# Window attention at one core: exponential out of PSUM, K spread by GpSimd, 32-column tiles, both pairs of windows weighed at once

## What is computed

```python
xn = layernorm(x)                         # over the 96 channels of a pixel
xw = windows(roll(xn, -4, -4))            # 4 windows of 8 x 8 = 64 tokens per image
q, k, v = split(xw @ qkv_w + qkv_b)       # 12 heads of 8 channels
attn = q * SCALE @ k.T + rel_bias + shift_mask     # 64 x 64 per window and head
out = softmax(attn) @ v                   # 12 heads side by side: 96 channels
x = x + unroll(out @ proj_w + proj_b)
```

## Time and profile before

| | before |
|---|---|
| time, median of 3 runs | 535.92 us |
| lowest and highest | 535.07, 537.8 us |
| profiled execution: span from first to last instruction | 540.4 us |
| TensorE busy | 518.1 us, 96% |
| VectorE busy | 365.9 us, 68% |
| ScalarE busy | 302.1 us, 56% |
| GpSimd busy | 178.3 us, 33% |

### The profile page before, as it was taken

How to read it: one execution, slowest core, us unless ns; L and a number is a source line. 1 busy time by engine, 2 the same in 40 slices (tenths; PEclk the granted TensorE clock), 3 DMA queues, 4 the chain that set the end, 5 groups by cost and what they waited for, 6 DMA issues and landing times. The chain is left out here.

```text
span 540.4 us, 23612 instructions
## 1 busy us (share of the span) xinstructions
PE 518.1 (96%) x9134; PEld 343.1 (63%) x9134; DVE 365.9 (68%) x1003; ACT 302.1 (56%) x763; POOL 178.3 (33%) x216
## 2 busy tenths in 40 slices
PE   7999999999999999998899999939999999999996
PEld 6777777777777777776674343339655655555553
DVE  1479999999999999997404354436556565656544
ACT  2278877777787778876435563103444444444432
POOL 8433444444434443344200220022433332333300
PEclk8599999999999999999999999957999999999999
DMA  4111111111111101100130132323454434444411
GB/s 83 29 42 32 30 30 46 29 30 30 30 29 24 26 24 29 29 3 2 45 75 21 46 93 71 88 49 79 121 146 124 115 101 118 121 114 105 117 51 32
DMA packets 41177, 32.51 MB, mean 60 GB/s; under 512 B 19240, under 2 KB 36776, under 8 KB 41128
## 3 DMA queue, kind: packets, MB, share of 16 engines
q1 hardware_dynamic: 37544, 26.11, 18.9%
q0 software_dynamic: 3584, 5.72, 4.8%
HBM read 18.36 MB, written 7.13 MB: 47 GB/s over the span
## 5 line engine op out<-in xcount | busy, mean ns | idle before, releaser
L383 POOL TENSOR_TENSOR scores<-scores,peak 128x768 f32<-128x768 f32 x64 | 94.3, 1473 | 135.3 <-DVE peak L552 135.3
L1224 POOL DMA_DIRECT2D x_stack<-padded_x x96 | 52.4, 548 | 97.4 <-PE ps_v L1497 63.4
L446 ACT COPY probs_t<-ps_probs 128x768 f32<-128x768 f32 x64 | 51.1, 799 | 40.7 <-PE ps_probs L706 40.7
L544 DVE TENSOR_TENSOR scores<-ps_scores,bias 128x768 f32<-128x768 f32 x64 | 61.3, 957 | 9.1 <-PE ps_scores L696 7.4
L552 DVE TENSOR_REDUCE peak<-scores 128x12 f32<-128x768 f32 x64 | 61.0, 953 | 2.4
L719 PE MATMUL ps_out<-v_blocks,probs_t 128*64 128x54 f32 x1536 | 57.2, 224 | 1.0 <-ACT out_t L451 0.9
L719 PEld LDWEIGHTS ps_out<-v_blocks,probs_t 128*64 128x64 f32 x1536 | 50.2, 138 | 12.3 <-issue 12.2
L706 PE MATMUL ps_probs<-ident,scores 128*128 128x128 f32 x384 | 55.0, 279 | 0.0
L440 ACT ACTIVATE scores<-scores 128x768 f32<-128x768 f32 x64 | 54.2, 846 | 0.6 <-POOL scores L383 0.6
L1037 ACT ACTIVATE hidden<-ps_hidden,fc_b_folded 128x512 f32<-128x512 f32 x48 | 29.1, 688 | 36.8 <-PE ps_hidden L978 36.8
L1497 PE MATMUL ps_qk<-x_stack,conv_w 40*32 40x256 f32 x1536 | 48.8, 379 | 0.0
(11 more groups left out here) (156 smaller groups left out, 900.2 us busy)
## 6 DMA issues: line engine op xcount, KB each, us to landing
x_stack<-padded_x SPq DMA_DIRECT2D x96, 54.0 KB
x_stack<-padded_x POOLq DMA_DIRECT2D x96, 54.0 KB, 2.7
padded_x<-x_pad SPq DMA_DIRECT2D x32, 121.5 KB, 2.5
x_sliced<-stream SPq DMA_DIRECT2D x48, 64.0 KB, 2.0
mixed<-y_sliced SPq DMA_DIRECT2D x48, 64.0 KB, 2.0
out<-y_sb SPq DMA_DIRECT2D x32, 96.0 KB, 2.0
x_now<-in_x SPq DMA_DIRECT2D x32, 72.0 KB, 1.8
stream<-in_x SPq DMA_DIRECT2D x32, 72.0 KB, 1.9
```

The source lines that it names most:

```text
L383: nc.gpsimd.tensor_tensor(sc, sc, peak[:, par, p, :].unsqueeze(2).to_broadcast((128, HEADS, WN)), ALU.subtract).then_inc(s["shifted"], 1)
L446: nc.scalar.copy(probs_t[:, :], ps_turned).then_inc(s["turned_copied"], 1)
L544: nc.vector.tensor_tensor(scores[:, par, p, :].rearrange("p (g c) -> p g c", g=NG), ps_scores[:, :, 0:GROUP * WN], bias[:, p, :].rearrange ...
L1224: engine.dma_start(x_stack[64 * half + i * HC:64 * half + (i + 1) * HC, slot, :, :], rows).then_inc(landed[slot], 16)
```

## The change

Part by part:

- **Exponential.** `exponent` and `copy_turned` become one instruction: the shifted scores are turned first, and Exp is applied on the way from `ps_turned` to `probs_t`.
- **K.** VectorE's `copy_k` is gone. ScalarE copies K with its bias to `k_sb`, and GpSimd's new `mask_k` spreads it to `k_blocks` (96 x 1024), which has two buffers now, as `q_sb` and `normed` have.
- **Tiles.** `make_v` is 16 matmuls with 32-column tiles in place of 8 with 64. `weigh` is 24 matmuls of 32 by 18 moving columns in place of 12 of 64 by 54.
- **Both pairs at once.** `ps_out` holds both pairs. One reciprocal (24 columns) and one product (192 columns) per image replace two of each half as wide; both turnings of heads follow each other.
- **Order.** TensorE: score(t+2,0), turn(t+1,0), make_v(t+2), turn_heads(t), turn_back(t+4), score(t+2,1), turn(t+1,1), weigh(t+1,0), make_k_and_q(t+4), turn_tokens(t+5), project(t), weigh(t+1,1). VectorE: invert_sums(t), weigh_heads(t), add_bias(t+2,0), find_peak(t+2,0), add_bias(t+2,1), measure(t+5), find_peak(t+2,1), gather_spread(t+5), add_residual(t). ScalarE: scale(t+4), exponent(t+1,0), copy_ot(t) twice, copy_v(t+2), copy_normed(t+4), exponent(t+1,1), copy_k(t+4), copy_q(t+4), inverse_deviation(t+5). GpSimd: subtract_peak(t,0), subtract_peak(t,1), mask_k(t+2). Steps now run from -6 to 31.

The core of the diff:

```diff
-    step(-4, -2, 0)
-    step(-3, -2, 1)
-    step(-2, -1, 0)
-    step(-1, -1, 1)
-    image_loop(engine, step, tail=2)
-    step(B, B // 2, 0)
+    for t in range(-6, 0):
+        step(t, t // 2, t % 2)
+    image_loop(engine, step, tail=3)
...
+        def mask_k(t, par):
+
+            pool.wait_ge(s["k_copied"], t + 1)
+            need(pool, s["scores_ready"], (t - 1) * 2)
+            nc.gpsimd.tensor_tensor(k_blocks[:, par, :, :], k_sb[:, :].unsqueeze(1).to_broadcast((C, GROUP, N)),
+                                    head_mask[:, :].unsqueeze(2).to_broadcast((C, GROUP, N)),
+                                    ALU.mult).then_inc(s["k_masked"], 1)
...
+        set_bias(0)
+        pool.wait_ge(consts_in, 16 * FIRST)
+        mask_k(0, 0)
+        set_bias(1)
+        mask_k(1, 1)
...
-            nc.scalar.copy(probs_t[:, :], ps_turned).then_inc(s["turned_copied"], 1)
+            nc.scalar.activation(probs_t[:, :], ps_turned, ACT.Exp).then_inc(s["probs_ready"], 1)
...
-        def make_q_and_k(t):
+        def make_k_and_q(t, par):
...
-            need(pe, s["biased"], t * 2)
+            need(pe, s["biased"], (t - 1) * 2)
...
-                for e in range(2):
-                    mm = nc.tensor.matmul(ps_v[64 * e:64 * e + 64, window, :, :], normed[:, window * WN:(window + 1) * WN],
-                                          heads[:, :, e, :], start=True, stop=True, skip_group_check=True)
+                for part in range(QUARTERS):
+                    at = window * WN + 32 * (part % 2)
+                    mm = nc.tensor.matmul(ps_v[32 * part:32 * part + 32, window, :, :], normed[:, par, at:at + 32],
+                                          heads[:, :, part // 2, :], start=True, stop=True, skip_group_check=True)
...
-                for top in range(2):
-                    mm = nc.tensor.matmul(ps_out[64 * top:64 * top + 64, 0, q * 2 * VC:(q + 3) * 2 * VC],
-                                          probs_t[:, q * 128 + 64 * top:q * 128 + 64 * top + 64],
-                                          v_blocks[:, par, p, top, q:q + 3, :, :].rearrange("p q e c -> p (q e c)"),
+                for part in range(QUARTERS):
+                    rows = slice(32 * part, 32 * part + 32)
+                    mm = nc.tensor.matmul(ps_out[rows, 0, at + q * 2 * VC:at + (q + 1) * 2 * VC],
+                                          probs_t[:, q * 128 + 32 * part:q * 128 + 32 * part + 32],
+                                          v_blocks[:, par, p, part // 2, q, :, :].rearrange("p e c -> p (e c)"),
                                           start=True, stop=True, skip_group_check=True)
...
             if is_image(t, -2):
-                fill(nc, free, blank[:, :], 10)
+                fill(nc, free, blank[:, :], 8)
...
+            if is_image(t, -3) or is_image(t, -2):
+                fill(nc, free, blank[:, :], 8)
```

More of the change, by code:

```diff
@@ L372, in _, with set_bias @@
         pool.wait_ge(second_in, 16 * SECOND)
-        for p in range(PAIRS):
+        def set_bias(p):
             nc.gpsimd.tensor_tensor(bias[:, p, :].rearrange("p (h m) -> p h m", m=WN),
@@ L434, in copy_v, with exponent @@
                 half = slice(64 * e, 64 * e + 64)
-                nc.scalar.copy(v_blocks[half, par, :, :, 0:HP, e, 0:HD].rearrange("p a b q d -> p (a b) q d"),
+                nc.scalar.copy(v_blocks[half, par, :, :, :, e, 0:HD].rearrange("p a b q d -> p (a b) q d"),
                                ps_v[half]).then_inc(s["v_copied"], 1)
[L438 to L442, removed]
+        def exponent(t, p):
             u = t * 2 + p
@@ L462, in step @@
                 token_deviation(nc, act, m, s2, 0)
+            if real(t + 4):
+                scale(t + 4)
             if real(t + 1):
[L464 to L471, removed]
+                exponent(t + 1, 0)
             if is_image(t, B - 2):
@@ L484, in step @@
             if real(t + 1):
-                copy_turned(t + 1, 1)
+                exponent(t + 1, 1)
+            if real(t + 4):
+                copy_k(t + 4)
+                copy_q(t + 4, par)
             if is_image(t, B - 2):
                 copy_tokens(nc, act, m, s2, 2, by_blocks(first_homes[2]))
+            if real(t + 5):
+                inverse_deviation(t + 5)
             if is_image(t, B - 1):
@@ L584, in step @@
         def step(t, half, par):
[L585 to L592, removed]
             if is_image(t, B - 2):
                 measure_tokens(nc, dve, m, s2, 0, by_blocks(first_homes[0]))
-            if real(t - 1):
-                add_residual(t - 1, half, par)
+            if real(t):
+                invert_sums(t)
+                weigh_heads(t)
             if is_image(t, B - 2):
@@ L604, in step @@
                 find_peak(t + 2, 0, par)
[L605 to L606 removed]
+                add_bias(t + 2, 1, par)
             if is_image(t, B - 2):
@@ L614, in step @@
                 measure_tokens(nc, dve, m, s2, 3, by_blocks(first_homes[3]))
[L615 to L619, removed]
+            if real(t + 5):
+                measure(t + 5)
+                await_stats(t + 5)
             if real(t + 2):
                 find_peak(t + 2, 1, par)
+            if real(t + 5):
+                gather_spread()
+            if real(t):
+                add_residual(t, half, par)
+            if is_image(t, -5):
+                prepare()
         def copy_slice(c):
@@ L769, in step @@
         def step(t, half, par):
-            last = is_image(t, B - 1)
-            if real(t - 1):
-                project(t - 1, 1 - par)
-            if real(t):
-                turn_heads(t, 0)
             if is_image(t, B - 2):
@@ L778, in step @@
             if real(t + 2):
-                make_q_and_k(t + 2)
-            if real(t):
-                weigh(t, 1, par)
+                score(t + 2, 0, par)
+            if is_image(t, -2):
+                fold_v()
             if real(t + 1):
@@ L795, in step @@
                 turn_first(3)
-            if last:
+            if is_image(t, B - 1):
                 fold_fc1(0)
@@ L801, in step @@
                 fold_fc1(2)
-            if is_image(t, -3):
-                fill(nc, free, blank[:, :], 8)
-            if real(t + 3):
-                turn_back(t + 3)
-            if real(t + 2):
-                make_v(t + 2)
             if real(t + 1):
+                turn(t + 1, 1, 1 - par)
                 weigh(t + 1, 0, 1 - par)
-            if is_image(t, -2):
-                fill(nc, free, blank[:, :], 4)
-            if real(t + 2):
-                score(t + 2, 1)
-            if real(t + 4):
-                turn_tokens(t + 4, half + 2, par)
-            if is_image(t, -3):
+            if is_image(t, -4):
+                turn_tokens(1, 0, 1)
                 fold_q_k_v()
@@ L819, in step @@
                 fill(nc, free, blank[:, :], 6)
-            if is_image(t, -2):
-                fill(nc, free, blank[:, :], 6)
+            if real(t + 4):
+                make_k_and_q(t + 4, par)
+            if is_image(t, -3) or is_image(t, -2):
+                fill(nc, free, blank[:, :], 8)
+            if real(t + 5) and not is_image(t, -4):
+                turn_tokens(t + 5, half + 2 + par, 1 - par)
+            if is_image(t, -5):
+                fill(nc, free, blank[:, :], 8)
+            if real(t):
+                project(t, par)
             if real(t + 1):
-                turn(t + 1, 1, 1 - par)
+                weigh(t + 1, 1, 1 - par)
         free = ps_probs[0:C, 0, 0:C]
```

125 lines of the change are left out of this document (64 added, 61 removed).

## The result

The changed kernel took 547.3 us (median of 4 executions, 546.6 to 548.6) against 536.9 for the kernel before (4 executions): a ratio of 1.018, interval 1.011 to 1.024. In a later comparison, with 12 executions against 16, the medians were 548.3 and 542.0 us; the ratio of 1.009 (1.002 to 1.016) that is on record for it takes from each kernel only the executions within 1.5% of its fastest. I had forecast 530.6 us and faster. Part of the distance is the clock of TensorE in the first 40 us, which differs from execution to execution.

A forecast was written before the change was run, and what follows sets the result against it. TensorE and VectorE were both taken as full. Steady state -7.8, start +2.5 and end 0 gave -5.3 us: 540.4 to 535.1 profiled, carried over to 530.6 us; range 521 to 541.

The forecast's parts named there:

- TensorE's sum, 6.61 us: TensorE's runs of one tile shape per image, each with its drain, add up to 6.61 us.
- The chain, 6.75 us: Once per image, tokens through VectorE to the bias, then TensorE's score to the next tokens: 3.4 plus 3.3 us, 6.75.
- my 5.4 us: VectorE's work per image after the change: about 5.4 of 7.02 us.
- I take a period of 6.75 us: 29 x (7.02 - 6.75) = 7.8: Steady state: time per image falls from 7.02 to 6.75 us, 7.8 us gained over 29 images.
- The start: Steps before the bias of image 2: 1.7 to 3.7 us more, taken at 2.5; bounds -2 and +4.
- The wait for GpSimd's mask: In the start, score(0,0) waits for the mask on GpSimd, at about 17 us.
- The end, 0: From the bias of image 31 on: same folds and token turnings in the same order, 0 within 0.5 us.
- I carry the difference over: From profiled span to median: the span stood 4.5 us above the 535.9 median, so 535.1 became 530.6 us.
- The first, 539 us: Rival: the wait at measure takes all VectorE gives up; chain 0.3 us longer, period 7.05, 539 us; chance 0.17.
- The third: Rival: small matmuls in make_v and weigh stay at 29 ns each, TensorE's sum 9.1 us, time 598; chance 0.04.
- ScalarE's Exp out of PSUM: ScalarE's Exp applied from PSUM, taken at 0.85 us, with bounds 0.80 and 1.0.
- the mask 1.89 (1.96): GpSimd's mask_k, 1024 columns: 1.96 us by the column ratio, 1.47 to 3 at the ends, covered by other work.

The follow-up runs named there:

- the two early profiles: Profiles of the changed kernel and the kernel before, each with TensorE's steps written out; medians 542.7 and 542.6 us, bias of image 2 at 36.78 and 30.81 us.
- the last variant: Changed kernel with TensorE written out, turn_tokens before make_k_and_q, no fills in steps -3 and -2, plus zero matmuls where TensorE idles early: 525.9 us, ratio 0.976.
- project last: Changed kernel with project moved behind the second weigh, last in TensorE's step: 537.5 and 552.3 us.
- tokens first: Changed kernel with turn_tokens ahead of make_k_and_q in TensorE's order: 534.9 to 548.2 us, ratio 0.998.
- fewer fills: Changed kernel without the zero matmuls of steps -3 and -2 (three fills of 8): 538.9 us.
- all three edits: Changed kernel with TensorE's steps written out, turn_tokens ahead of make_k_and_q, and no fills in steps -3 and -2: 530.6 us, ratio 0.989.

## Why the prediction was wrong, step by step

- **TensorE's sum, 6.61 us: right.** The terms came out as weigh 0.54 (forecast 0.53), make_v 0.47 (0.52), four turnings 0.58 (0.57), K to project 1.63 (1.66), turn 0.80, and score 0.60 and 0.64 (0.60 twice). That the whole fits to 0.01 is partly luck: make_v was 0.05 too dear and one score 0.04 too cheap. The reading that a change of shape drains, and that both engines were full, held: relieving TensorE alone stopped at VectorE's 6.85.
- **The chain, 6.75 us: right in kind, 0.1 too short.** It limits the step without an edge, with the wait at the moments where I put it (1.5 us, I wrote 1.3). Beside an edge that step takes 6.72 to 6.81, but with the edge gone the steps take 6.80 and 6.91, 6.86 in the mean. Images 2 to 31 took 197.0 us against my 195.8; that they are so near is partly luck, since the last two of them take 5.8 and 5.9 us. VectorE was busy for 0.73 of a steady stretch, where I wrote near 0.8: my 5.4 us had its 0.25 of idle time in it.
- **"I take a period of 6.75 us: 29 x (7.02 - 6.75) = 7.8" failed on an omission.** The edge of TensorE's loop has no term in it. Of the 0.30 us by which the period of 7.05 is off, 0.19 are the edge's and 0.11 the chain's. The edge costs 5.1 us here and next to nothing before. The kernel before has steps of 7.01 and 7.05 us in turn, so its loop costs nothing that shows; I did not ask what hides it, although the change puts a run of short matmuls in that place.
- **The start, "taken at 2.5": wrong in size.** It cost 5.8 us (6.0 in the two early profiles). I priced the fills at 2.7 us each, as they came out (2.8), but 3.9 us go when all three are left out, more than my whole 2.5. The wait for GpSimd's mask, which I named, did not count: the mask is ready at 16.9 us and the score starts at 20.7, behind the tokens and a fill. The rest, 1.9 us, was not taken apart; the lower clock lasted some 9 us longer in the changed kernel's profile, which may be cause or consequence.
- **The end, 0:** 0.3 us.
- **"I carry the difference over": wrong.** A span mostly lies 1.7 us under its execution's time (544.9 and 546.6 here), so the profiled execution of the kernel before took some 542 us: one whose clock rose late (0.963 in the mean), against a median of early ones. The changed kernel's rises late more often than not. By the spans I was 9.8 us too low (535.1 against 544.9), by the medians 16.7.
- **Which rival came closest?** The first, 539 us, by its arithmetic (nothing back in the steady part, the start lost), but not by its mechanism: the chain was longer by 0.1 us and not by 0.3, and the rest was the loop's edge. The third, small matmuls at 29 ns each, is ruled out. ScalarE's Exp out of PSUM took 0.81 us and the mask 1.89 (1.96).

The sum in short: forecast -7.8 + 2.5 + 0 = -5.3 us; profiled -1.6 + 5.8 + 0.3 = +4.5 us; and the lot of the start between the medians.

## What to carry to other kernels

Give the edge of a hardware loop a line of its own in the sum, and ask what work TensorE has in hand there; moving one pair of long matmuls behind the short ones, or writing the loop out, gave back most of it here. Where two engines are full and each change of tile shape drains, add up TensorE's runs from load to load: the terms were good to 0.05 us each. Make the parts of a large change alone as well: the 32-column tiles by themselves, in the kernel before, gave a lower median than all but the last variant. And before spans are turned into medians, look at the clock of the start in several executions.

## What the runs showed of the hardware that I had not expected

- Weights on 32-column tiles cost about 11 ns a record in a run of 48, drain included (0.54 us), those on 64-column tiles 34 ns (0.81 for 24), and 18 or 54 moving columns make hardly any difference to the latter (0.81 against 0.84).
- TensorE can stand without work for 0.6 us at a loop's edge (1.15 from load to load in place of 0.55), with nothing named in the trace and no packet in the instruction queue between 100 and 200 us. What happens in that time stays open.
- Zero matmuls at the lower clock are not a sure way to the upper one: 24 of them (48 records) in the changed kernel's steps -3 and -2 left the clock low until 38 us (0.74 in the mean from 25 to 50 us), and without them it rose at 37 (0.76). Whether they help in other executions is open: of the 26 executions with these fills and tiles (the changed kernel, written out, project last, tokens first) six had a mean clock of 0.975 to 0.979, and of the ten without the fills (fewer fills, all three edits) none had more than 0.970.
